# A chunked-attention first block: loads, normalisation, query masks and the softmax inverse moved between engines and queues

## The reference, cut to what matters

```python
x = L0_attn_hidden_states                # (8, 512, 128)
xn = layernorm(x)                        # no gain, no bias
s = chunked_attention(xn, ...)           # 8 heads of 16, chunks of 12 queries, 24 keys
g = silu(six_layer_transformer(xn, ...))
return x + s * g
# chunked_attention: q, k, v = xn @ Wq.T, xn @ Wk.T, xn @ Wv.T
#   q *= Q_SCALE * softplus(per_dim_scale);  k *= K_SCALE
#   logits = q.k (24 keys of context) + rel_shift(q . (pos @ Wrel.T))
#   logits = tanh(logits / 50) * 50;  attn = softmax(logits);  out = attn.v @ Wpost.T
```

## Time and profile before

| | us |
|---|---|
| median of 3 runs (range) | 3797.96 (3797.13 to 3800.81) |
| profiled execution: its time / its span | 3794.33 / 3792.6 |
| first block: projections / bias / loop | 46.5 / 27.1 / 153 |
| PE clock in the bias stage (share of full) | 0.94 |
| rest of the program, 228.8 to 3792.6 | 3563.8 |

### The profile page before, as it was taken

The page is one execution under the profiler, slowest core; times in us unless marked ns, Lnnn a source line. Parts: engine busy times, 40 slices in busy tenths (PEclk is TensorE's granted clock), DMA queues, the critical chain, the costliest instruction groups (busy, mean ns, idle before and its releaser), DMA issues. The chain is left out here.

```text
span 3792.6 us, 150168 instructions
## 1 busy us (share of the span) xinstructions
PE 3308.5 (87%) x64584; PEld 2479.7 (65%) x64970; DVE 2844.1 (75%) x3988; ACT 2302.5 (61%) x4617; POOL 2253.0 (59%) x1982
## 2 busy tenths in 40 slices
PE   7848899888899889899889889889889988999985
PEld 3736666666666666666666666666667666666663
DVE  5348778777777787877877877878777787777783
ACT  4326666666656666666666666666666666666664
POOL 0037666666666666666666666666666666666661
PEclk9769999999999999999999999999999999999998
DMA  1021011011111011111101101101101011110112
GB/s 30 20 71 37 28 31 31 28 29 59 31 29 31 28 29 59 31 29 31 31 27 59 32 28 31 29 29 60 31 28 31 29 31 56 30 32 28 30 30 71
DMA packets 94827, 133.97 MB, mean 35 GB/s; under 512 B 21065, under 2 KB 45152, under 8 KB 93280
## 3 DMA queue, kind: packets, MB, share of 16 engines
q1 hardware_dynamic: 86508, 123.78, 11.0%
q10 hardware_dynamic: 7668, 0.50, 0.2%
HBM read 25.60 MB, written 4.26 MB: 8 GB/s over the span
## 5 line engine op out<-in xcount | busy, mean ns | idle before, releaser
L1022 POOL TENSOR_TENSOR qs<-rprod 128x512 f32<-128x512 f32 x768 | 993.6, 1303 | 843.2 <-DVE rprod L1092 827.8
L1092 DVE TENSOR_TENSOR rprod<-ps,tab 128x1024 f32<-128x1024 f32 x768 | 923.0, 1219 | 402.9 <-PE ps L779 315.6
L1033 POOL TENSOR_TENSOR qs<-qs,rr 128x512 f32<-128x512 f32 x768 | 805.7, 1070 | 276.7 <-ACT rr L964 276.7
L777 PE MATMUL ps<-wh,xls 128*128 128x512 f32 x1152 | 587.2, 510 | 50.8 <-PEq L733 39.7
L828 PE MATMUL ps<-pt,v 64*64 64x32 f32 x24768 | 443.6, 221 | 184.6 <-ACT pt L954 181.7
L828 PEld LDWEIGHTS ps<-pt,v 64*64 64x64 f32 x24768 | 400.1, 135 | 262.8 <-ACT pt L954 227.9
L788 PE MATMUL ps<-con,qs 128*128 128x128 f32 x3080 | 513.6, 290 | 0.0
L942 ACT ACTIVATE sq<-ps 128x512 f32<-128x512 f32 x384 | 228.4, 595 | 441.7 <-PE ps L779 437.7
L1038 POOL TENSOR_TENSOR pr<-pr,rinv 128x512 f32<-128x512 f32 x386 | 403.1, 1044 | 124.8 <-DVE rinv L1134 124.2
L807 PE MATMUL ps<-kT,qT 64*32 64x64 f32 x24704 | 423.7, 218 | 57.5 <-DVE gx L1140 0.8
L1110 DVE TENSOR_REDUCE ssq<-sq 128x16 f32<-128x1024 f32 x384 | 464.0, 1208 | 0.0
(11 more groups left out here) (159 smaller groups left out, 5005.2 us busy)
## 6 DMA issues: line engine op xcount, KB each, us to landing
v<-v SPq DMA_DIRECT2D x384, 192.0 KB
v<-v SPq DMA_DIRECT2D x288, 64.0 KB
raw<-in_L_ffn_Wqkv SPq DMA_DIRECT2D x7, 1536.0 KB, 7.4
wo<-in_L_ffn_Wo SPq DMA_DIRECT2D x6, 512.0 KB, 8.8
sT<-so SPq DMA_DIRECT2D x22, 96.0 KB, 1.6
bias<-in_L_attn_hidden_states SPq DMA_DIRECT2D x8, 256.0 KB, 5.6
srow<-sT SPq DMA_DIRECT2D x8, 256.0 KB, 3.3
xrow<-in_L_attn_hidden_states SPq DMA_DIRECT2D x8, 256.0 KB, 4.0
```

The costliest lines, as they stand in the source:

```text
L777: nc.tensor.matmul(dst, al, bh, start=True, stop=False)
L1022: nc.gpsimd.tensor_tensor(qs[:, i % 2, j].rearrange("p (h s d) -> p h s d", s=2, d=HALF), prod[:, 0, j].rearrange("p (h s d) -> p h s d", ...
L1033: nc.gpsimd.tensor_tensor(q3, q3, rr[:, 8 * j:8 * j + 8].unsqueeze(2).broadcast_to([P, 8, DH]), ALU.mult).then_inc(cur["mul"], 1)
L1092: return nc.vector.tensor_tensor(prod[:, :, j, :].rearrange("p c (h d) -> p c h d", d=DH), ps[:, bank, :].rearrange("p (h d) -> p h d", d= ...
```

## The change

In the projections: ScalarE's queue loads its function table first, then `pds` in one broadcast DMA with its own semaphore, then `con`, Wq, Wrel and the positions; SyncE's queue loads Wk, Wv and Wpost between the batches. GpSimd normalises, and copies batch b-1 to `cx` behind the normalisation of batch b. ScalarE copies the raw queries once into a new tile `qr` (two buffers), and VectorE makes all four masked copies from there. ScalarE takes the deviation of batch 3, and the residual copies of batches 0 and 1, ahead of the weights; the deviation of batch b+4 stands behind the keys of batch b-1. TensorE turns batches 0 and 1 ahead of the weights.

In the loop: the output projection stands behind the values and writes to bank 2; the spread inverses go to banks 0 and 1 (which the scores use) as 32 products of 48 columns by 48 rows instead of 16 of 96 by 96; the sums become 8 products instead of 4. The copy to `so` stands behind exp and the values' copy. The scores of group g wait for `s_mul` of group g-2. The core of the diff (lines removed are, for the most part, left out; they stand in the listing above):

```diff
+                if b in (1, 2, 3):
+                    i = (WK, WV, WP)[b - 1]
+                    sp.dma_start(wnat[:, i, :], t[names[i]]).then_inc(d_w, 16)
...
+            for b in range(B + 1):
+                if b < B:
+                    pool.wait_ge(s_rs, b + 1)
+                    for k in range(TB):
+                        nc.gpsimd.tensor_scalar(xnat[:, b, k, :], xnat[:, b, k, :], mv[:, b, k, 0:1],
+                                                rstd[:, b, k:k + 1], ALU.subtract, ALU.mult).then_inc(s_xn, 1)
...
+                j = b - 1
+                if j >= 0:
...
+                    nc.gpsimd.tensor_copy(cx[:, j * BT + CCH:j * BT + CCH + S], xT[:, j, :]).then_inc(s_cx, 1)
...
-            dve.wait_ge(d_w, 16 * (6 + CH))
+            dve.wait_ge(d_pds, 16)
...
             statistics(1)
...
+            dve.wait_ge(d_w, 16 * 6)
...
-                    for m in (2, 3):
-                        last = nc.vector.tensor_scalar(q4[:, m, j * BT:j * BT + S], ps[:, 2 + j % 2, :], head(m), None,
-                                                       ALU.mult)
...
+                for m in range(4):
+                    last = nc.vector.tensor_scalar(q4[:, m, j * BT:j * BT + S], qr[:, j % 2], head(m), None, ALU.mult)
...
+                    p4 = pe_[:, j % 4].rearrange("p (u a n) -> p a u n", u=GQ, a=2)
+                    nc.vector.tensor_tensor(p4, p4, ps[:, 0:2, 0:48 * GQ].rearrange("p a (u n) -> p a u n", u=GQ),
+                                            ALU.mult).then_inc(s_mul, 1)
...
+            nc.scalar.preload_act_table_set(LN_EXP)
+            act.dma_start(pds[:, 0:1], t["L0_attn_per_dim_scale"].rearrange("(a d o) -> a d o", a=1, o=1)
+                          .broadcast_to([CH, CD, 1])).then_inc(d_pds, 16)
+            act.dma_start(con[:], t["consts"]).then_inc(d_con, 16)
+            for i in (WQ, WR):
+                act.dma_start(wnat[:, i, :], t[names[i]]).then_inc(d_w, 16)
             act.dma_start(pos[:], t["L0_attn_position_embeddings"]).then_inc(d_w, 16)
...
+            deviation(3)
...
+            residual(0)
+            residual(1)
...
+                    if j >= 2:
+                        act.wait_ge(s_qd, j - 1)
...
-                    for m in (0, 1):
-                        last = nc.scalar.activation(q4[:, m, j * BT:j * BT + S], ps[:, 2 + j % 2, :], ACT.Copy,
-                                                    scale=head(m))
...
+                    nc.scalar.copy(qr[:, j % 2], ps[:, 2 + j % 2, :]).then_inc(s_qa, 1)
...
+                if b + 4 < B:
+                    deviation(b + 4)
...
+                                   ps[:, 2, 0:GW].rearrange("p (s u q) -> p s u q", s=4, q=CCH)) \
...
+            turn(0)
+            turn(1)
...
+            for b in range(B):
+                if b >= 1 and b + 1 < B:
+                    turn(b + 1)
+                project(b)
...
+                    if g >= 2:
+                        pe.wait_ge(s_mul, g - 1)
...
+                    if j >= 3:
+                        pe.wait_ge(s_pv, j - 2)
...
+                        for a in range(2):
+                            last = nc.tensor.matmul(ps[64 * a:64 * a + 48, 2, col:col + 4],
+                                                    pe_[:, j % 4, u * 96 + a * 48:u * 96 + a * 48 + 48],
+                                                    con[:, C_ON:C_ON + 4], start=True, stop=True,
+                                                    skip_group_check=True, tile_position=(0, 64 * a))
...
+                j = g - 3
+                if j >= 0:
+                    pe.wait_ge(s_oa, j + 1)
+                    pe.wait_ge(s_od, 3 * (j + 1))
+                    if g - 1 < NG:
+                        pe.wait_ge(s_rec, g)
+                    nc.tensor.matmul(ps[:, 2, 0:GW], wT[:, WP, :], ob[:, j % 2], start=True, stop=True,
+                                     skip_group_check=True).then_inc(s_po, 1)
...
+                    pe.wait_ge(s_add, min(g + 1, NG))
...
+                            for a in range(2):
+                                last = nc.tensor.matmul(
+                                    ps[32 * s:32 * s + 32, a, u * 48:u * 48 + 48],
+                                    rc[64 * a:64 * a + 48, j % 2, 4 * u + s:4 * u + s + 1].broadcast_to([48, 32]),
+                                    ident[64 * a:64 * a + 48, 64 * a:64 * a + 48], start=True, stop=True,
+                                    skip_group_check=True, tile_position=(64 * a, 32 * s))
...
-                        pe.wait_ge(s_pv, j)
+                        pe.wait_ge(s_oa, j)
+                        pe.wait_ge(s_od, 3 * j)
...
```

More of the change, by code:

```diff
@@ L297, in _ @@
             nc.vector.tensor_scalar(pds[:, 3:4], pds[:, 2:3], 1.0, None, ALU.add).then_inc(s_sp, 1)
-            normalise(1)
+            statistics(2)
             dve.wait_ge(s_sp, 4)
@@ L301, in _ @@
                                            op0=ALU.max, op1=ALU.add).then_inc(s_sp, 1)
-            statistics(2)
             dve.wait_ge(s_sp, 5)
+            dve.wait_ge(d_w, 16 * 6)
             nc.vector.tensor_scalar(wqs[:], wnat[:, WQ, :], pds[:, 5:6], Q_SCALE, ALU.mult, ALU.mult).then_inc(s_wq, 1)
-            for b in range(2, B + 4):
+            for b in range(3, B + 4):
                 if b < B:
-                    normalise(b)
-                if b + 1 < B:
-                    statistics(b + 1)
+                    statistics(b)
                 if b == 4:
@@ L341, in _ @@
                     dve.wait_ge(s_su, j + 1)
-                    nc.vector.reciprocal(rc[:, j % 2], ps[0:96, 2, 384:400]) \
-                        .then_inc(s_rec, 1)
+                    nc.vector.reciprocal(rc[0:112, j % 2], ps[0:112, 2, 384:400]).then_inc(s_rec, 1)
                     dve.wait_ge(s_bc, j + 1)
-                    nc.vector.tensor_tensor(pe_[:, j % 4], pe_[:, j % 4], ps[:, 2, 0:96 * GQ], ALU.mult) \
-                        .then_inc(s_mul, 1)
+                    p4 = pe_[:, j % 4].rearrange("p (u a n) -> p a u n", u=GQ, a=2)
+                    nc.vector.tensor_tensor(p4, p4, ps[:, 0:2, 0:48 * GQ].rearrange("p a (u n) -> p a u n", u=GQ),
+                                            ALU.mult).then_inc(s_mul, 1)
                 j = g - 2
@@ L386, in _, with residual @@
             deviation(2)
+            deviation(3)
+            def residual(b):
+                act.wait_ge(s_tr, b + 1)
+                nc.scalar.copy(xT[:, b, :], ps[:, b % 2, :]).then_inc(s_xt, 1)
+            residual(0)
+            residual(1)
             for i in range(5):
@@ L391, in _ @@
             for b in range(B + 1):
-                if b < B:
-                    act.wait_ge(s_tr, b + 1)
-                    nc.scalar.copy(xT[:, b, :], ps[:, b % 2, :]).then_inc(s_xt, 1)
-                if 3 <= b + 3 < B:
-                    deviation(b + 3)
+                if 2 <= b < B:
+                    residual(b)
                 if b >= 1:
@@ L418, in _ @@
                     nc.scalar.activation(pe_[:, g % 4], pe_[:, g % 4], ACT.Tanh, scale=1.0 / SOFTCAP).then_inc(s_th, 1)
+                if g < NG:
+                    act.wait_ge(s_th, g + 1)
+                    nc.scalar.activation(pe_[:, g % 4], pe_[:, g % 4], ACT.Exp, scale=SOFTCAP).then_inc(s_ex, 1)
+                    act.wait_ge(s_vp, g + 1)
+                    nc.scalar.copy(vs[:, g % 4].rearrange("p u d -> p (u d)"), ps[:, 3, :]).then_inc(s_ve, 1)
                 j = g - 3
@@ L462, in _ @@
             nc.tensor.transpose(ps[:, 7, P:P + NPOS], pos[:], ident[0:NPOS, 0:NPOS]).then_inc(s_wt, 1)
-            turn(0)
             pe.wait_ge(s_we, 6)
             nc.tensor.matmul(ps[:, 7, 256:256 + NPOS], wT[:, WR, :], posT[:], start=True, stop=True).then_inc(s_rl, 1)
-            for b in range(1, B):
-                turn(b)
-                project(b - 1)
-            project(B - 1)
+            for b in range(B):
+                if b >= 1 and b + 1 < B:
+                    turn(b + 1)
+                project(b)
             pe.wait_ge(s_qa, B)
@@ L511, in _ @@
                     pe.wait_ge(s_ex, j + 1)
-                    if j >= 1:
-                        pe.wait_ge(s_mul, j)
+                    if j >= 3:
+                        pe.wait_ge(s_pv, j - 2)
                     if j == 0:
```

58 lines of the change are left out of this document (11 added, 47 removed).

## The result

The changed kernel takes 3821.05 us (median of 6 runs, 3817.07 to 3829.09), the kernel before 3799.39 beside it (6 runs, 3797.13 to 3808.81): a ratio of 1.0053 [1.0038, 1.0068]. I had forecast 3777, with a range of 3756 to 3796. Rival 3, the supply of instructions, to which I gave 0.09, is what happened. That its total of 3818 came within 3 us is luck: it was made up of 25 us more in the loop and 5 less in the projections, and the rows show 14 more in the loop's 19 iterations, 0.6 more in the projections and a slower rest.

What follows compares the result with a forecast made beforehand. TensorE was taken to set the loop's pace, a load to bind the projections' start. Projections -5, bias 0, loop -16, its ends 0: -21 from 3794.33 gives 3773.3; median 3.6 higher, so 3777, range 3756 to 3796.

Steps and rivals of the forecast that it cites:

- Rival 3: Loop: 20 more instructions an iteration starve TensorE; period 7.9, loop 25 us longer, total near 3818; chance 0.09.
- The loop's period, 5.75: Loop: mean of 4.9 us at full clock (60%) and 7.0 at half (40%), saving 16 us over 19 iterations.
- the one at full clock: Loop: an iteration at full clock was to take 4.9 us, 0.35 less than before.
- Its threshold, 6.85: Loop: mean period in us above which the loop's loss would exceed the projections' 5 us gain.
- The clock, 40% at full to 60%: Loop: halved idle time was to raise the share of full clock from 40 to 60%.
- The inverses, 0.77 at full clock: Loop: 32 products of 48 columns were to take 0.77 us, against 0.79 for the old inverses.
- The moved projection, 0.35 at full clock: Loop: values placed in TensorE's wait ahead of the output projection were to shorten the full-clock period by 0.35 us.
- The wait for `s_mul`: Loop: the scores' new wait was to be hidden by some 0.2 us, bare only in iteration 2, 0.8 once.
- The projections, -5: Projections stage: bias stage was to start at 41.3 us against 46.5, 5 us less.
- the ring: Projections: raw queries, masks, statistics, deviation and residual copy wait on each other in turn; about 5.0 us, three times.
- GpSimd's normalisation: Projections: 1.4 us a batch, at most 2.4, was to stay ahead of the 5.0 us ring.
- The ports: Projections: VectorE's masks might wait for GpSimd on shared ports, costing 4 us, nearly all of that stage's gain.

Runs made afterwards that it cites:

- i: Kernel before plus one 512-column product per iteration in TensorE's wait ahead of the output projection, its result overwritten; ratio 1.0032 to the kernel before.
- d: Kernel before plus 20 products of the scores' form per iteration ahead of the output projection, results overwritten (484 rows); ratio 1.0034 to the kernel before.
- e: Kernel before with inverses as 4 products instead of 16 (reciprocal copied 32 times over) and the output projection behind the values; ratio 1.0048.
- f: Kernel before with inverses as 4 products instead of 16 (reciprocal copied 32 times over), output projection still ahead of the values; ratio 1.0060.
- c: Kernel before with only the inverses split into 32 products and the sums into 8, output projection still ahead of the values; ratio 1.0069.
- b: Kernel before with only the output projection moved behind the values (still bank 4) and the copy to `so` later; ratio 1.0002.
- g: Kernel before with the change's projections part, but VectorE normalising and GpSimd only copying `cx`; loop as before; one run, 3800.04 us.
- m: Same program as g, timed in rounds against the kernel before: 3794.69 us (11 runs), ratio 0.9983.

## Why the prediction was wrong

- **The loop's period, 5.75: the step that failed.** I summed durations of steps and asked only which semaphore comes last. The rival of the supply was set aside with "gaps are rare, and an iteration at 4.9 still has 0.35 us of wait to take some up". But the gap of the earlier trace rows comes just behind an iteration that had used 404 rows in 5.24 us, 3.3 us for 256. The forecast period asked for 484 rows in 5.75, 3.0 us for 256, and the one at full clock for 2.6, on average over 19 iterations. What can be had is 3.84 to 3.88, for where TensorE has run dry, the next piece is fetched only after it has gone on, and is of use some 3.8 us later. Even with 404 rows that is a floor of 6.1 (an estimate from these paces), not far below the 6.585 of before, so the whole reserve of the loop was 9 us, where I sought 16 to 31. The rival was priced too high (a period of 7.9, measured 7.317) since the gaps were added to an iteration at half clock; they take the place of slow stretches. Its threshold, 6.85, was right. (Scores, sums and values, given as 2.45, add up to 2.48; nothing hangs on it.)
- **The clock, 40% at full to 60%.** It fell, from 0.78 to 0.66. i shows the reasoning half right: with the wait filled it rises to 0.89. But the changed kernel has more idle time than before, 21.8 us against 13.7, only elsewhere. And in d, e, f and i clock and period don't go together.
- **The inverses, 0.77 at full clock.** Right: 0.75. These rows are the inverses at full clock and the group that follows:

```profile
135.93 0.80 PE L560 MATMUL ps<-con,rc 48*32 48x48 f32 x64
136.68 0.68 PE L576 MATMUL ps<-probs,vs 24*64 24x48 f32 x40
```

  At half clock the row is 1.02 long (188.23) instead of 1.51. The sums gained too: 0.53 where the earlier trace rows has 0.84. The split makes both of its steps shorter, and still the loop of c takes 12.7 us more in 19 iterations. The rule of the Trainium skill (TensorEngine Tiling, Instruction Overhead), a floor of about 60 columns for a product, would have had 0.99; the measurement doesn't bear the figure out, yet its advice not to cut a small dimension holds, for another reason.
- **The moved projection, 0.35 at full clock.** 0.13 over the loop in one profile (b), none in the medians.
- **The wait for `s_mul`.** Hidden, as said: one wait of 0.6 from 80 to 200 us.
- **The projections, -5.** The load, the ring and the masks came out: the first query product at 16.15 (14.7), raw queries of batches 0 to 3 on ScalarE 4.5 us apart (5.0), four masks 1.74 (1.7). The raw queries of the last four batches took 12.6 instead of 8.4. The term that was mis-sized is GpSimd's normalisation: 3.1 to 4.4 a batch, where I took 1.4 and as an upper bound 2.4. The bound came from a copy (L272), which has no arithmetic and reads no operand per partition; which of the two costs the time, no run separates. The Trainium skill (GPSIMD Engine Reference, Engine selection) says of GpSimd's elementwise work that "1-input is roughly line-rate"; here one such instruction is 902 ns against VectorE's 348. With VectorE in its place most of the predicted gain is there (41.8 in g, 43.9 in m, the same program; predicted 41.3).
- **The ports.** VectorE's masks took 512 ns beside GpSimd's normalisation and 502 without it (g), so the 4 us of that argument were not lost on VectorE's side; GpSimd's instruction is 799 ns at the median, and 1022 to 1328 where it runs beside three or four masks.

## What to carry to other kernels

Before a product is split, count the instructions: rows of matmul and weight load in a period, times the pace at which the trace's densest stretches were ever fed, is a floor of its own beside work and waits. A gap put down to issue in the midst of equal instructions is that floor showing; count the rows from one to the next, and look in the DMA records for packets of kind instruction that end just before. If the distances are multiples of one number, each instruction added costs its share (here 15 ns a row) once the floor is reached, short as it may be. For an operation that a trace lacks on an engine, take the upper bound from a row that has the same kind of operands and arithmetic, not from a copy.

## What the hardware showed

- TensorE's instructions arrive in pieces of 256, rows and semaphore instructions together; where it ran dry, a piece took 3.3 to 4.2 us from gap to gap, 3.84 to 3.88 in the mean of three loops, at a granted clock of 0.50 as of 1.00. Its fetch is one packet of 16384 bytes that lasts 0.9 to 1.5 us, starts 1.0 us or more after TensorE has gone on from a gap, and is of use 1.1 to 1.6 us after its end. A gap lasts 0.2 to 2.2 us in the first block, up to 3.9 behind it.
- The granted clock is 0.66 in the mean of a loop with no gap of issue and TensorE busy for 94% (f, 132.29 of 140.34 us); with a long product in the wait it is 0.89 (i), with twenty short ones 0.86 (d), where before it is 0.78.
- Four float32 products of 96 columns with 96 x 128 weights take 2.02 us at half clock and 1.13 at full (f), sixteen with a quarter of the weights each 1.51 and 0.86 (before).
- GpSimd's subtract and multiply of 128 columns with two values per partition: 0.79 to 1.33 us; on VectorE 0.33 to 0.35 in the mean.
